# Softmax attention of the third block: ScalarE's work in three lists, value product transposed in four column groups, row sums by a matrix of ones

## The reference, cut to what matters

```python
def _mha(x, Wqkv, bqkv, Wo, bo):          # D = 128, H = 4 heads, hd = 32
    S, B, _ = x.shape                      # x is (8, 512, 128): attention runs over S = 8
    hd = D // H
    qkv = x @ Wqkv.T + bqkv
    q, k, v = jnp.split(qkv, 3, axis=-1)
    ...
    scores = jnp.einsum('bhqd,bhkd->bhqk', q, k) * (1.0 / np.sqrt(hd))
    att = jax.nn.softmax(scores, axis=-1)
    o = jnp.einsum('bhqk,bhkd->bhqd', att, v)
    ...
    return o @ Wo.T + bo
y = _layer_norm(x + _mha(x, Wqkv, bqkv, Wo, bo), g1, be1)
idx = jnp.argmax(xf @ Wg.T, axis=-1)       # in _moe: the row's expert, one of 8
```

## Time and profile before

| what | value |
|---|---|
| median of three runs | 3414.5 us (3413.73 to 3419.38) |
| the profiled execution, its own time | 3416.19 us |
| its span in the profile | 3414.4 us |
| the stage of the change, from the first load of its input to the first instruction of the next stage | 1277.80 to 1569.58 us, 291.8 us |
| granted TensorE clock, mean over the span | 0.822 of full speed |
| granted TensorE clock, mean over the stage | 0.61 |
| TensorE, VectorE, ScalarE, GpSimd busy in the stage | 188, 112, 73, 78 us |

### The profile page before, as it was taken

One profiled execution on the slowest core, in us unless ns is written; L12 is line 12 of the kernel. 1 busy time (PEld: TensorE's weight loads), 2 busy tenths in 40 slices (PEclk: granted clock), 3 DMA queues, 4 the chain that ended last, 5 costly groups with the idle time before them and its releaser, 6 DMA issues. The chain is left out here.

```text
span 3414.4 us, 49243 instructions
## 1 busy us (share of the span) xinstructions
PE 2524.0 (74%) x17446; PEld 1269.1 (37%) x17454; DVE 2234.6 (65%) x4562; ACT 1497.3 (44%) x2911; POOL 1138.9 (33%) x1172
## 2 busy tenths in 40 slices
PE   3999987874898876775557777677624846899986
PEld 1333334442444445554522222222214842233334
DVE  4888868784667644342368887888742237888854
ACT  1777761110555542222344444444311214777751
POOL 3222104432221202232435555555573433222001
PEclk9999997775899986556877877777856976999989
DMA  5111100000211201005800000000014942212100
GB/s 161 32 39 28 31 1 0 1 0 19 42 31 38 45 25 39 14 19 169 255 9 1 0 0 0 0 0 1 0 35 158 292 145 43 48 30 41 20 4 22
DMA packets 129156, 157.01 MB, mean 46 GB/s; under 512 B 18000, under 2 KB 110288, under 8 KB 128304
## 3 DMA queue, kind: packets, MB, share of 16 engines
q1 hardware_dynamic: 119248, 139.91, 15.7%
q0 software_dynamic: 6592, 13.56, 1.1%
q10 hardware_dynamic: 3072, 0.40, 0.1%
HBM read 95.56 MB, written 25.59 MB: 35 GB/s over the span
## 5 line engine op out<-in xcount | busy, mean ns | idle before, releaser
L422 DVE TENSOR_REDUCE a_mx<-banks 128x1 f32<-128x512 f32 (+3 forms) x1536 | 882.6, 618 | 253.3 <-PE banks L762 123.1
L633 ACT ACTIVATE a_prob<-banks 128x512 f32<-128x512 f32 (+3 forms) x1536 | 773.9, 545 | 382.4 <-PE banks L785 156.9
L785 PE MATMUL banks<-a_Qs,a_Ks 64*128 64x512 bf16 (+3 forms) x1536 | 512.6, 368 | 48.1 <-ACT a_prob L633 40.9
L762 PE MATMUL banks<-a_Ks,a_Qs 63*128 63x512 bf16 (+3 forms) x1536 | 503.1, 375 | 45.7 <-DVE a_mx L422 32.7
L813 PE MATMUL banks<-a_prob,a_vaug 128*32 128x256 f32 (+2 forms) x5632 | 446.3, 390 | 0.7 <-ACT a_prob L633 0.5
L2073 PE MATMUL banks<-m_hc,kc 128*128 128x512 f32 x512 | 340.5, 765 | 118.5 <-POOL m_hc L1949 99.5
L1949 POOL TENSOR_TENSOR m_hc<-m_h,m_cs 128x512 f32<-128x512 f32 x256 | 327.9, 1297 | 287.0 <-DVE m_h L1813 274.7
L1996 ACT ACTIVATE banks<-m_dt,acoef 128x512 f32<-128x512 f32 x256 | 175.8, 691 | 297.2 <-DVE m_h L1813 296.9
L1813 DVE TENSOR_TENSOR_SCAN m_h<-banks,m_u 128x512 f32<-128x512 f32 x256 | 301.6, 1209 | 0.0
L762 PEld LDWEIGHTS banks<-a_Ks,a_Qs 63*128 63x128 bf16 x1536 | 126.7, 95 | 406.0 <-DVE a_mx L422 220.7
L1798 DVE TENSOR_TENSOR m_u<-m_dtx,banks 128x1024 f32<-128x1024 f32 x128 | 155.3, 1213 | 104.6 <-PE banks L2054 102.0
(11 more groups left out here) (405 smaller groups left out, 4730.3 us busy)
## 6 DMA issues: line engine op xcount, KB each, us to landing
c_wbuf<-in_w2e SPq DMA_DIRECT2D x71, 512.0 KB, 4.2
b_wbuf<-in_w1e SPq DMA_DIRECT2D x39, 578.0 KB, 4.4
a_Ks<-a_parts SPq DMA_DIRECT2D x288, 64.0 KB
a_Qs<-a_parts SPq DMA_DIRECT2D x288, 64.0 KB
rows_in<-in_unused SPq DMA_DIRECT2D x1, 4579.5 KB, 16.7
c_yb<-rows_in SPq DMA_DIRECT2D x71, 64.5 KB, 4.8
a_mixed_in<-rows_back SPq DMA_DIRECT2D x16, 256.0 KB, 3.9
a_Qs<-a_negm ACTq DMA_DIRECT2D x192, 2.0 KB
```

The lines of the kernel that those rows point to most:

```text
L422: dve.tensor_reduce(mx[:, g % 2, col:col + 1], M[:, k % 3, 0:keys[j]], AX.X, ALU.max).then_inc(S("max_read"), 1)
L633: act.activation(prob[:, n % 8, first_query[kt]:T], Sc[:, n % 2, first_query[kt]:T], ACT.Exp, scale=scale).then_inc(S("exped"), 1)
L762: i = pe.matmul(M[:, k % 3, 0:keys[j]], Qs[lo:lo + LAST, b % 4, pair, j * P:(j + 1) * P], Ks[lo:lo + LAST, b % 4, pair, 0:keys[j]], start= ...
L785: i = pe.matmul(Sc[:, n % 2, q0:T], Ks[lo:lo + HALF, b % 4, pair, kt * P:(kt + 1) * P], Qs[lo:lo + HALF, b % 4, pair, q0:T], start=True, s ...
```

## The change

The weighted sum of values is computed transposed. Before, the transposed probabilities were the stationary operand and 33 columns of `vaug` moved past them. Now a head's 32 columns of `v_sb` are the stationary operand, 512 columns of `pT` move past in four pieces of 128, and the head's output lands in 32 of the 128 partitions: four heads, four column groups of the array, one bank ("AV", 16 matmuls a unit). The row sums come from 16 more matmuls of the same form, with 32 columns of ones as the stationary operand ("SUM"); they land in the same layout, each sum repeated over the head's 32 partitions. VectorE takes the reciprocal of the whole bank of 128 by 512 ("recip") and multiplies ("oT"); the product already is `oT`. The transposition of `o`, its copy and the two small reciprocals and multiplications are gone. `pT` has room for two whole units, and SUM starts when all four heads of the unit are copied out.

ScalarE's work is now in three lists: copies, exponentials and copies of `pT`, so that due times decide how they mix. `UNIT` is 22.0 and all due times are new. Sorted by them, the orders are:

TensorE: SUM.a, AV.a, y.b, q.b, out.a, k.b, v.b, scores.b, hold.a, tp0.b, tp1.b, logits.a, tp2.b, tp3.b, counts.a, SUM.b.

ScalarE: hT.b, qT.b, kT.b, exp0.b, exp1.b, exp2.b, h2T.a, pT0.b, exp3.b, pT1.b, pT2.b, pT3.b.

VectorE: recip.a, oT.a, acc.a (L1352 and statistics), v.b, h.a, mx0.b to mx3.b, the statistics of unit c, route.a, slots.a, y.c, recip.b.

GpSimd: reciprocal deviation for h.a, hold.a, deviation for y.c, scatter.a, base.c.

The banks `M` go in turn to SUM and AV, y and q, out and k, v and hold, logits and counts: ten uses a unit before and after.

```diff
-                vaug = room("vaug", [P, 2, NT, SH, SD + 1])
-                prob, pT = room("prob", [P, 2, SH, T]), room("pT", [P, 4, T])
+                v_sb, ones = room("v", [P, 2, NT, C]), room("ones", [P, SD])
+                prob, pT = room("prob", [P, 2, SH, T]), room("pT", [P, 2, SH, T])
...
-                UNIT = 17.0
-                MARKS = {"y": 6.0, "q": 8.5, "k": 10.0, "v": 11.5, "av0": 22.5, "av1": 26.5, "o": 30.0, "out": 32.5,
-                         "hold": 43.0, "logits": 45.5, "counts": 48.5}
+                UNIT = 22.0
+                MARKS = {"y": 6.0, "q": 8.5, "k": 10.0, "v": 11.5, "sum": 26.3, "av": 27.0, "out": 31.0,
+                         "hold": 41.0, "logits": 43.5, "counts": 46.5}
...
-                        yield t + 16.5 + 1.2 * head
+                        yield t + 16.2 + 0.9 * head
...
-                    for pair in range(2):
-                        name = "av%d" % pair
-                        yield t + (25.7, 29.0)[pair]
-                        wait_written(dve, name, n)
...
-                        link(dve, dve.reciprocal(rden[:, r, pair], av[:, :, :, SD]))
-                        read(dve.tensor_tensor(o[:, r, :, pair * 64:(pair + 1) * 64].rearrange("p t (h d) -> p t h d", h=2),
-                                               av[:, :, :, 0:SD], rden[:, r, pair].unsqueeze(3).broadcast_to([P, NT, 2, SD]),
-                                               ALU.mult), name, n)
-                    yield t + 31.5
-                    wait_written(dve, "o", n)
...
-                    read(dve.tensor_copy(oT[:, r, :], M_of("o", n)), "o", n)
-                    yield t + 34.0
+                    yield t + 28.0
+                    wait_written(dve, "sum", n)
+                    if n:
+                        wait_read(dve, "av", n - 1)
+                    read(dve.reciprocal(rden[:, :], M_of("sum", n)), "sum", n)
+                    yield t + 29.0
+                    wait_written(dve, "av", n)
+                    wait_read(dve, "sum", n)
+                    if n >= 2:
+                        wait_written(dve, "out", n - 2)
+                    read(dve.tensor_tensor(oT[:, r, :], M_of("av", n), rden[:, :], ALU.mult), "av", n)
+                    yield t + 32.6
...
+                def scalar_exps(act, n):
+                    t, r = begin(n), n % 2
                     for head in range(SH):
-                        yield t + 17.6 + 2.0 * head
+                        yield t + 17.4 + 1.15 * head
...
+                def scalar_turned(act, n):
+                    t, r = begin(n), n % 2
+                    for head in range(SH):
+                        yield t + 20.7 + 1.5 * head
+                        act.wait_ge(S("p_turned"), SH * n + head + 1)
...
+                        act.activation(pT[:, r, head, :], Pt[:, head % 2, :], ACT.Copy).then_inc(S("pT_ready"), 1)
...
-                        yield t + 19.5 + 2.0 * head
+                        yield t + 19.5 + 1.5 * head
...
+                    for name in ("sum", "av"):
+                        yield t + MARKS[name]
+                        wait_free(pe, name, n)
+                        if name == "sum":
+                            pe.wait_ge(S("pT_ready"), SH * (n + 1))
+                            wait_read(pe, "v", n)
+                            pe.wait_ge(S("ones_set"), 1)
                         for j in range(NT):
-                            at = (j * 2 + head % 2) * (SD + 1)
-                            i = pe.matmul(M_of(name, n)[:, at:at + SD + 1], pT[:, m % 4, j * P:(j + 1) * P],
-                                          vaug[:, r, j, head, :], start=True, stop=True)
...
+                            for head in range(SH):
+                                lo = SD * head
+                                left = ones[:, :] if name == "sum" else v_sb[:, r, j, lo:lo + SD]
+                                i = pe.matmul(M_of(name, n)[lo:lo + SD, j * P:(j + 1) * P], left,
+                                              pT[:, r, head, j * P:(j + 1) * P], start=True, stop=True)
+                        written(i, name, n)
...
-                    yield t + MARKS["o"]
-                    wait_free(pe, "o", n)
-                    wait_read(pe, "av0", n)
-                    wait_read(pe, "av1", n)
-                    written(turn(pe, o[:, r], M_of("o", n)), "o", n)
```

More of the change, by code:

```diff
@@ L1217, in units_all @@
                 xall, hold = room("xall", [P, B, NT, C]), room("hold", [P, B, NT, ROW])
-                y, base, o, h = (room(n, [P, 2, NT, C]) for n in ("y", "base", "o", "h"))
+                y, base, h = (room(n, [P, 2, NT, C]) for n in ("y", "base", "h"))
                 hT, oT, h2T, qkT = room("hT", [P, 2, T]), room("oT", [P, 2, T]), room("h2T", [P, 2, T]), room("qkT", [P, 2, 2, T])
-                vaug = room("vaug", [P, 2, NT, SH, SD + 1])
-                prob, pT = room("prob", [P, 2, SH, T]), room("pT", [P, 4, T])
+                v_sb, ones = room("v", [P, 2, NT, C]), room("ones", [P, SD])
+                prob, pT = room("prob", [P, 2, SH, T]), room("pT", [P, 2, SH, T])
                 stats, mom, small = room("stats", [P, 2, NT, 6]), room("mom", [P, 2, 2, NT, 2]), room("small", [P, 2, 2, 2, NT])
-                mx, neg, rden = room("mx", [P, 2, SH, NT]), room("neg", [P, 2, SH, NT]), room("rden", [P, 2, 2, NT, 2])
+                mx, neg, rden = room("mx", [P, 2, SH, NT]), room("neg", [P, 2, SH, NT]), room("rden", [P, T])
                 best, first, slot = (room(n, [P, NT]) for n in ("best", "first", "slot"))
@@ L1285, in vector_set @@
                                     wb("ids").bitcast(I32).unsqueeze(2)).then_inc(S("numbered"), 1)
-                    dve.memset(vaug[:, :, :, :, SD:SD + 1], 1.0).then_inc(S("ones_set"), 1)
+                    dve.memset(ones[:, :], 1.0).then_inc(S("ones_set"), 1)
                 def vector_pre(dve, n):
@@ L1310, in vector_pre @@
                     wait_written(dve, "v", n)
-                    dve.wait_ge(S("ones_set"), 1)
                     if n >= 2:
-                        wait_written(dve, "av1", n - 2)
-                    read(dve.tensor_tensor(vaug[:, r, :, :, 0:SD],
-                                           M_of("v", n).rearrange("p (j h d) -> p j h d", j=NT, h=SH),
-                                           wb("bv").rearrange("p (h d) -> p h d", h=SH).unsqueeze(1).broadcast_to([P, NT, SH, SD]),
-                                           ALU.add), "v", n)
+                        wait_written(dve, "av", n - 2)
+                    read(dve.tensor_tensor(v_sb[:, r], tiles(M_of("v", n)), rep(wb("bv")), ALU.add), "v", n)
                 def vector_core(dve, n):
@@ L1359, in vector_post @@
                     i.then_inc(S("moments2"), 1)
-                    yield t + 38.0
+                    yield t + 36.6
                     dve.wait_ge(S("rstd2"), n + 1)
@@ L1370, in vector_route @@
                     t, row = begin(n), [P, NT, E8]
-                    yield t + 46.5
+                    yield t + 44.6
                     wait_written(dve, "logits", n)
@@ L1410, in gpsimd_unit @@
                     gp.tensor_tensor(base[:, r], y[:, r], rep(wb("bo")), ALU.add).then_inc(S("base_ready"), 1)
-                    yield from norm(gp, t + 36.3, 1, n, "moments2", "rstd2")
-                    yield t + 39.5
+                    yield from norm(gp, t + 35.0, 1, n, "moments2", "rstd2")
+                    yield t + 37.8
                     gp.wait_ge(S("normed2"), n + 1)
@@ L1436, in scalar_unit @@
                         read(act.activation(qkT[:, r, i, :], M_of(name, n), ACT.Identity, bias=wb("cols")[:, i:i + 1]), name, n)
+                    yield t + 42.2
+                    wait_written(act, "hold", n)
+                    if n >= 2:
+                        wait_written(act, "logits", n - 2)
+                    read(act.activation(h2T[:, r, :], M_of("hold", n), ACT.Copy), "hold", n)
+                def scalar_exps(act, n):
+                    t, r = begin(n), n % 2
                     for head in range(SH):
-                        yield t + 17.6 + 2.0 * head
+                        yield t + 17.4 + 1.15 * head
                         act.wait_ge(S("negmax"), SH * n + head + 1)
@@ L1445, in scalar_unit @@
                         i.then_inc(S("exped"), 1)
-                        yield t + 20.3 + 2.0 * head
-                        m = SH * n + head
-                        act.wait_ge(S("p_turned"), m + 1)
-                        if m >= 4 and head % 2 == 0:
-                            act.wait_ge(S("av_even"), m // 2 - 1)
-                        if m >= 4 and head % 2:
-                            wait_written(act, "av%d" % (head // 2), n - 1)
-                        act.activation(pT[:, m % 4, :], Pt[:, m % 2, :], ACT.Copy).then_inc(S("pT_ready"), 1)
-                    yield t + 44.3
-                    wait_written(act, "hold", n)
-                    if n >= 2:
-                        wait_written(act, "logits", n - 2)
```

(6 more changed lines are left out.)

24 lines of the change are left out of this document (5 added, 19 removed).

## The result

The changed kernel took 3357.14 us in the median of four runs (3349.86 to 3365.53), the kernel before 3415.35. The ratio is 0.9829, 95% interval 0.9803 to 0.9855. I had forecast 3376 with a range of 3362 to 3389. The direction was right, and the gain was 58 us where I had 38.

The account below looks back on a forecast made before the run. Bound by a chain of TensorE's order with waits between steps. First SUM at 1306.0, seven periods 191.8, drain 33.5: stage ends at 1531.3, 38.3 us earlier; 3414.5 - 38.3 = 3376, range 3362 to 3389.

Parts of the forecast that it names:

- the walk: One period from SUM to SUM, step by step with durations from rows: 28.9 us at lower clock, 27.4 forecast.
- 0.22 of the upper level: Clock over a period: granted 0.61 kept from before, meaning the upper level for 0.22 of the time.
- 6.7 us between the levels: One period: 28.9 us at the lower level against 22.2 at the upper; 5.7 saved up to scores, 1.0 after.
- the rival on the clock: TensorE busier per period loses upper-level time; lower level throughout gives 28.9 us periods and 3387; chance 0.14.
- more upper clock: TensorE's granted clock above 0.70 in the periods: 3363; chance 0.06.
- New SUM and AV: TensorE's new matmuls: 32 records each, overlapping in column groups, 2.08 us each, 4.16 for both.
- the rival of a slower kernel: Column groups don't overlap: SUM and AV take 14.0 us together, kernel 24 us slower, 3439; chance 0.04.
- Reciprocal: VectorE's reciprocal of 512 elements a partition ahead of y: 3.33 us, by 6.2 ns an element.
- The price of the stall: TensorE's wait for the reciprocal ahead of y: as cheap as a copy, 1.3 us less each, 3366; chance 0.03.
- The run of products: TensorE from y to v, back to back: q 1.91, out 2.05, k 1.91, v 2.07 us at the lower clock.
- The maxima: VectorE between scores and exponentials: all four maxima run together, 0.93 us from maximum to exponential.
- The tail: Exponentials to next SUM: hangs on ScalarE at the upper level, which saves only 1.0 us there.

Follow-up runs that it names:

- e_fill: The changed kernel with the AV matmuls issued twice, same result: 3332.2 us, ratio 0.9752.
- e_order: The kernel before with only the new order of the queues, old value product and transposition of o kept: 3349.7 us, ratio 0.9803.
- b_fill: The kernel before with five unused bfloat16 matmuls ahead of the first and second transposition of each unit: 3407.8 us, ratio 0.9982.
- three single fillings: The changed kernel with AV twice (3332.2 us), five unused matmuls behind AV (3347.6), or eight between scores and hold's transposition (3352.3).
- two fillings: The changed kernel with AV issued twice and eight unused matmuls between scores and hold's transposition: 3351.1 us, ratio 0.9820.
- e_yfirst: The changed kernel with the next unit's y ahead of SUM on TensorE: 3343.1 us; with AV also issued twice: 3344.7 us.
- e_product: The kernel before with only the new value product and sums by ones, in the old order: 3378.6 us, ratio 0.9890.

## Why the prediction was wrong, by its steps

The period is where the error lies, so I take the walk's four pieces, in the mean over seven periods of the first trace. "At lower" is the walk at the lower level, "forecast" has its 0.22 of the upper level in it.

| piece of a period, us | at lower | forecast | measured |
|---|---|---|---|
| SUM's start to y's start | 5.5 | 5.5 | 6.1 |
| y's start to the scores' end | 13.5 | 12.2 | 9.65 |
| to the first exponential | 1.0 | 1.0 | 1.6 |
| to the next SUM | 8.9 | 8.7 | 7.9 |
| sum | 28.9 | 27.4 | 25.3 |

- **The clock: the step that failed.** "The pattern of work and idle stretches is alike, so I keep it" put the upper level on 0.22 of the time. It was 0.46 (granted 0.73). By the prediction's own 6.7 us between the levels that is 1.6 us a period, 11 us of the 16 missing; with it the forecast would have been near 3365, inside the range. Most of it lies from y to the scores, where the granted clock was 0.71 and the time 2.6 us below the forecast. e_fill, with 1.0 there, takes 7.4 us, and the walk's upper level had 7.8. And the rival on the clock had the wrong sign: "TensorE is busier per period, which can cost upper-level time", 0.14 for it against 0.06 for more upper clock, which had a price, 3363, near the result, but no reason.
- **Why the clock rose** from 0.61 to 0.73 is shown in part. Each half of the change raises it alone, the order to 0.69 and the product to 0.71, and work put into TensorE's waits raises it within one kernel. But TensorE's busy share is 70% in both kernels and 61% with the product alone, so the idle share doesn't explain the rise; which property of order and product does, no run settles.
- **New SUM and AV.** They overlap in column groups, as forecast: 32 records in 1.93 us, so the rival of a slower kernel fell. But in five of the seven periods the reciprocal started 2.9 us after SUM's first record, not 2.13 (1375.94 to 1378.90 in the period shown), in the other two 2.0 and 2.2. The records put SUM's end at 1.93 in both cases; they don't show the last matmul's true end there. Cost: 0.6 us a period in the mean that I did not have.
- **Reciprocal.** 3.36 us against 3.33. The line through the three sizes of the earlier trace rows held to 512 elements. The wait ahead of y was 2.8 to 3.0 us in five of seven periods and 1.9 in two, not 1.4, for the same late start and a faster AV.
- **The price of the stall.** I had a copy in its place at 1.3 us a period; it was 4.1 to 4.9. The step took SUM and AV at the lower level as the next limit, and no effect of a stall on what follows it.
- **The run of products.** At the lower level q, out, k and v follow each other at 1.84, 1.71 and 1.71 us (1383.83 to 1389.09), where I had 1.91, 2.05 and 1.91: the durations of rows overlap when nothing waits between. 0.6 us a period less, a part of the 2.6 that isn't the clock's.
- **The maxima.** I had VectorE free when the scores end. They now end while it is at `h`, or just behind it, so the first exponential starts 1.6 us after them, not 1.0. Cost: 0.6 us a period.
- **The tail** (exponentials, h2T, `pT`, transpositions, hold) went in the walk's order and took 7.9 us, 0.7 less than forecast and about what the walk gives it at the upper level throughout; the clock was 0.75 from the scores to SUM. hold was ready at the first exponential's end (both 1368.70 in the period before the one shown), where I had it 1.0 us ahead.
- **What I did not ask.** Which of the two edits the gain hangs on. The walk priced the product's effect as real; e_order shows that the order alone has it all. The sign of the forecast would have been right without the product, so it is no evidence for the product's part in the walk.

The four pieces give 2.1 us a period or 14.7 us; 1.3 more are the way to the first SUM and the drain, and the remaining 4 us of the 20 are within the scatter outside the stage. What stays open: the part of the piece from y to the scores that neither the clock at the walk's own price (5.7 us for 0.20 more of the upper level, 1.1) nor the spacing of products (0.6) gives, some 0.9 us; when the reciprocal starts 2.0 us after SUM and when 2.9; and the gaps inside a doubled AV. The level falls and rises at moments that shift against the period; I have one trace of each kernel but two of the changed one, and don't settle on a story.

## What to carry to other kernels

Price a chain at both clock levels and ask, for each wait of TensorE, what stands behind it: here the wait for the reciprocal cost its length and then the clock of the run of products behind it. Doing both halves of a change apart is worth two runs; here one half, the order of the queues, gave all of it, and the other moved work from TensorE into a 3.4 us reciprocal on the path. A higher mean of the granted clock is no gain by itself; it pays only in stretches that end in TensorE.

## What the runs showed of the hardware

- A reciprocal of 512 float32 a partition takes 3.36 us on VectorE, a copy of the same tile 0.69 us.
- The same group of products (q, out, k) took 4.2 to 5.5 us in the changed kernel, where y waited for 1.9 to 3.0 us ahead of it, and 3.0 us in all periods of e_fill, where y waited for 0.6 to 1.8 us.
- More work in TensorE's waits went with a higher granted clock in every kernel tried: 0.61 to 0.69 (b_fill), 0.73 or 0.77 to 0.79, 0.81 and 0.82 (the changed kernel, two traces, and its three single fillings), 0.85 with two fillings, 0.69 to 0.79 (e_order) and 0.77 to 0.81 (e_yfirst). The 0.79 alone is within the 0.04 between the two traces.
- The granted clock doesn't follow the busy share across kernels: 0.61 at 70% (before), 0.71 at 61% (e_product), 0.69 at 85% (e_order).
- VectorE's `neg` of 4 elements a partition took 0.17 us alone and 0.54 to 0.56 us beside GpSimd's multiplication (L1405) and addition (L1406) for `hold`, as in these rows of the changed kernel; the maxima between them stayed at 0.68 to 0.69 us. That GpSimd is the cause is read from their overlap, no run removes it.

```profile
1366.44 1.09 POOL L1405 TENSOR_TENSOR u_h<-u_h,w_b 128x512 f32<-128x512 f32 x1 [1.23 <-DVE u_h L1356]
...
1367.00 0.56 DVE L1323 TENSOR_SCALAR u_neg<-u_mx 128x4 f32<-128x4 f32 x1
...
1367.61 1.09 POOL L1406 TENSOR_TENSOR u_hold<-u_h,w_b 128x512 f32<-128x512 f32 x1
...
1368.18 0.55 DVE L1323 TENSOR_SCALAR u_neg<-u_mx 128x4 f32<-128x4 f32 x1
...
1369.35 0.17 DVE L1323 TENSOR_SCALAR u_neg<-u_mx 128x4 f32<-128x4 f32 x1
```
